# Decoder recurrence on one Trainium2 core: the shifted table of alignments, the place of the state term, and who adds the mask

## The chip, the core and the metric

One NeuronCore of a Trainium2 chip runs the whole program: a chain of eight layers over 16 rows of 128 tokens. The metric is the device time of one execution, in microseconds (us). The change touches only the decoder recurrence, a loop of 128 steps that lie behind each other.

## What is computed

The decoder reads the encoder rows `hbatch` (16 batches, 128 positions) and makes 128 steps. Each step needs the attention weights `alpha` and the state `s` of the step before:

```python
def step(carry, tgt):
    s, c, alpha = carry
    f = lax.conv_general_dilated(alpha, conv_w, (1,), 'SAME', dimension_numbers=('NCH', 'OIH', 'NCH'))
    e = jnp.einsum('a,bta->bt', va, jnp.tanh(enc_proj + (s @ Wa_s.T)[:, None, :] + jnp.einsum('bft,af->bta', f, Wa_f) + ba))
    e = jnp.where(mask, e, jnp.float32(-1e+30))
    alpha_new = jax.nn.softmax(e, axis=1)[:, None, :]
    g = jnp.einsum('bt,btd->bd', alpha_new[:, 0], hbatch)
    y = jnp.tanh(g @ L_gy_w.T + L_gy_b + s @ L_sy.T) @ L_yy_w.T + L_yy_b
    rec = tgt @ L_ys.T + s @ L_ss.T + g @ L_gs_w.T + L_gs_b
    ig, fg, cg, og = jnp.split(rec, 4, axis=1)
    c_next = _sig(fg) * c + _sig(ig) * jnp.tanh(cg)
    s_next = _sig(og) * jnp.tanh(c_next)
    return ((s_next, c_next, alpha_new), y)
```

`conv_w` has 10 filters of 101 taps over the 128 positions; the mask cuts off positions beyond a batch's length. The output `y` is made after the loop from saved states and weights.

## The kernel before, in words

Everything here is in `stage_decoder`. The 16 batches are two groups (`g` = 0, 1) of 8. The loop `steps` runs 64 times over two time steps; a time step is two halves, `half(g, n, o, m, ...)`. In a half, group `g` does the back of its step n (context, gates, state) while the other group `o` does the front of its step (convolution, tanh, energies, softmax). So there are 256 halves, and each group goes round once in two of them. Every engine has its own copy of `half` and runs its instructions in the order in which they are written there; semaphores tie the engines together.

One half, by engine and line of the profile:

- TensorE (PE): `turn_alignment` (L1839) turns the weights `al` of group g into `AT`; `state_term` (L1781) makes `Wa_s` times the state of o into `SW`; `spread_filters` (L1800) adds the 10 filters, spread over 128 channels by `Wa_f`, to the sums that hold the encoder part; `gates_of_context` (L1828) makes the gates of g, in two parts with `mask` (L1808) between them, which starts the energies `E` of o with the mask through an identity matrix in bf16; `energy` (L1815) adds the energies; `turn_gates` (L1835) turns `rec` into `T`; `gates_of_state` (L1821) begins the gates of o; `filter_rows` (L1789) applies the filters of g's next step to the table `hk`, two batches to each of the four 32-column tiles of the array.
- ScalarE (ACT): `keep_filters` (L1883) copies the filtered rows out of PSUM, times `ri`; `squash` (L1893, L1898) is the tanh over 8 batches; `fill` (L1886) puts the encoder part into PSUM for g's next step; L1912 is the tanh of g's gates; `exps` (L1902) is the exponential of the energies of o with its row sum, which a second instruction reads out; L1916 is the tanh of the cell.
- VectorE (DVE): `keep_alignment` (L1990), `keep_state_term` (L1963), `add_state` (L1973), `fill` (L1967), the gate sum `rec` (L2004), `top` (L1980: the negated row maximum of the energies), the cell (L2010, L2012, L2013), `align` (L1984: the reciprocal `ri` of the row sum; L1985: `al` = `ex` times `ri`), and last the state `sT` (L2021).
- SyncE (SP), the DMA queue: it writes the exponentials of o to DRAM, padded with 50 zeros in front (L1748, 4 KB), waits for that to land, and reads them back as the table `hk` (L1750): row t, batch b holds the padded row shifted by t, so that 101 shifted copies (padded to 112 rows) stand under each other and a matmul over the rows is the convolution. In the second time step of an iteration it also loads the next `rin` (L1754).
- GpSimd (POOL) stores weights and states for the output.

The order around the change is thus written out by hand; no planner decides it. The table of o, made from the exponentials of one half, is used by `filter_rows` at the end of the next.

## Time and profile before

| | us |
|---|---|
| median of 3 runs | 4053.48 (4051.23 to 4054.08) |
| the profiled execution, its own time | 4058.55 |
| its span | 4056.8 |
| decoder loop in it, first to last gate tanh | 2201.6 to 3566.0 |

Over the span TensorE is busy 80%, its weight loads 54%, VectorE 55%, ScalarE 39%, GpSimd 12%. The page cuts the span in 40 slices; the decoder loop is slices 22 to 35, in which the granted TensorE clock is 9 tenths or more. Busy shares tell little in such a loop: what counts is which wait ends last in each half. Of a row of the timeline the first number is the start in us from the start of the span, the second how long it took; in square brackets stands the idle time of the engine before it and what ended it.

### The profile page before, as it was taken

The page shows a single profiled execution, that of the slowest core. Times are in us where ns is not written, and L with a number is a line of the kernel's source. Part 1 is how long each engine was busy: PE and PEld are TensorE (multiplying, and loading weights), DVE is VectorE, ACT ScalarE, POOL GpSimd, SP SyncE. Part 2 cuts the span into 40 slices and gives each one's busy share as a digit, 9 for nine tenths or more (in the row PEclk, how much of TensorE's full clock was granted, in tenths as well). Part 3 has the DMA queues.
Part 4 walks back from the last instruction along what each step waited for, and adds up shares of the span by engine and source line. Part 5 has one row for each costly group of instructions (what it writes and reads, how often), then busy time and mean ns, then how long its engine had stood idle before and what let it go on. Part 6 is the DMA issues. An engine that isn't in the chain of part 4 may idle for free. (4 is left out here: it accounts for less than half of the span.)

```text
span 4056.8 us, 109059 instructions
## 1 busy us (share of the span) xinstructions
PE 3261.3 (80%) x43050; PEld 2192.1 (54%) x43122; DVE 2232.7 (55%) x5373; ACT 1577.2 (39%) x3966; POOL 505.4 (12%) x1854
## 2 busy tenths in 40 slices
PE   7556568544489999998598999999999999965998
PEld 4424145322266666666354666666666666623554
DVE  2656767588845555555213555555555555563444
ACT  2221134344422222222112666666666666622222
POOL 0000421233300000000000000000000000033222
PEclk8576689877789999999798999999999999975888
DMA  2000020200010000000101333333333333301000
GB/s 95 3 3 0 10 46 9 86 0 0 0 44 0 0 0 0 0 0 0 52 26 50 90 90 90 90 90 88 91 89 90 90 90 87 93 18 48 25 26 31
DMA packets 278734, 176.56 MB, mean 44 GB/s; under 512 B 14320, under 2 KB 267840, under 8 KB 278608
## 3 DMA queue, kind: packets, MB, share of 16 engines
q1 hardware_dynamic: 275920, 172.57, 14.5%
q0 software_dynamic: 2752, 3.18, 0.5%
q8 instruction: 37, 0.61, 0.1%
q14 instruction: 25, 0.20, 0.0%
HBM read 164.98 MB, written 13.90 MB: 44 GB/s over the span
## 5 line engine op out<-in xcount | busy, mean ns | idle before, releaser
L1828 PE MATMUL ps<-de_hg,st_at 128*32 128x128 f32 x16384 | 516.3, 275 | 0.3 <-DVE st_at L1990 0.3
L1828 PEld LDWEIGHTS ps<-de_hg,st_at 128*32 128x32 f32 x16384 | 424.5, 110 | 31.6 <-DVE st_at L1990 0.5
L1893 ACT ACTIVATE st_th<-ps,st_sw 128x128 f32<-128x128 f32 x1024 | 292.8, 369 | 248.0 <-PE ps L1800 248.0
L1973 DVE TENSOR_TENSOR st_th<-ps,st_sw 128x512 f32<-128x512 f32 x256 | 177.2, 692 | 155.1 <-PE ps L1800 155.1
L1247 PEld LDWEIGHTS ps<-sa_xt,w_wq 128*128 128x128 f32 x2048 | 234.7, 194 | 11.1 <-issue 9.3
L1247 PE MATMUL ps<-sa_xt,w_wq 128*128 128x128 f32 x2048 | 237.9, 278 | 2.0 <-ACT sa_xt L1363 2.0
L1766 POOL COPY de_ah<-st_at 128x8 f32 (+1 forms) x256 | 51.1, 199 | 1507.0 <-DVE st_at L1990 1507.0
L1318 PE MATMUL ps<-sa_wo,sa_ct 128*128 128x512 f32 x512 | 225.0, 598 | 13.1 <-issue 13.1
L1789 PE MATMUL ps<-st_hk,st_cwt 112*32 112x128 f32 x4096 | 164.7, 278 | 84.9 <-DMA st_hk<-padded_alignments 82.9
L2228 PE MATMUL ps<-rf_wb,rf_sp 128*128 128x512 bf16 x737 | 202.2, 434 | 4.7 <-issue 2.9
L1800 PE MATMUL ps<-st_fs,st_waf 32*128 32x128 f32 x4096 | 186.5, 296 | 12.2
L1789 PEld LDWEIGHTS ps<-st_hk,st_cwt 112*32 112x32 f32 x4096 | 100.6, 109 | 149.6 <-ACT st_gt L1912 106.6
L1967 DVE COPY ps<-de_enc 128x512 f32<-128x512 f32 x256 | 175.1, 684 | 5.3 <-PE ps L1862 5.3
L955 PE MATMUL ps<-w_identb,ff_q 128*128 128x128 bf16 x256 | 33.1, 311 | 173.8 <-ACT ff_q L1000 173.8
L2004 DVE TENSOR_TENSOR st_rec<-ps,st_rin 128x128 f32<-128x128 f32 x256 | 74.8, 292 | 176.2 <-PE ps L1828 176.2
L1318 PEld LDWEIGHTS ps<-sa_wo,sa_ct 128*128 128x128 f32 x512 | 96.6, 191 | 135.2 <-issue 135.2
L1815 PE MATMUL ps<-st_th,st_vas 128*32 128x128 f32 x4096 | 165.0, 279 | 1.9 <-ACT st_th L1898 1.9
L1898 ACT ACTIVATE st_th<-st_th 128x512 f32<-128x512 f32 x256 | 165.3, 646 | 0.0
L1886 ACT COPY ps<-de_enc 128x512 f32<-128x512 f32 x256 | 157.1, 613 | 12.9 <-PE ps L1862 12.9
L121 ACT ACTIVATE X<-sa_row,sa_rs_ln 128x1024 f32 (+1 forms) x16 | 19.9, 1242 | 343.0 <-POOL sa_rs_ln L117 343.0
L1800 PEld LDWEIGHTS ps<-st_fs,st_waf 32*128 32x128 f32 x4096 | 137.7, 185 | 26.8 <-ACT st_fs L1883 23.9
L2228 PEld LDWEIGHTS ps<-rf_wb,rf_sp 128*128 128x128 bf16 x768 | 84.2, 113 | 114.1 <-issue 49.9
(410 smaller groups left out, 6456.5 us busy)
## 6 DMA issues: line engine op xcount, KB each, us to landing
st_hk<-padded_alignments SPq DMA_DIRECT2D x254, 448.0 KB, 3.6
X<-in_x_dram SPq DMA_DIRECT2D x16, 512.0 KB, 9.2
out_dram<-X SPq DMA_DIRECT2D x16, 512.0 KB, 2.7
w_wq<-in_Wq_perm_dram SPq DMA_DIRECT2D x1, 4096.0 KB
sa_wo<-in_Wo_perm_dram SPq DMA_DIRECT2D x1, 4096.0 KB, 14.2
gate_inputs<-dp_ro SPq DMA_DIRECT2D x16, 256.0 KB, 2.3
st_rin<-gate_inputs SPq DMA_DIRECT2D x128, 32.0 KB, 3.3
rf_wf<-in_weightT_dram SPq DMA_DIRECT2D x8, 512.0 KB, 4.3
```

The source lines that it names most:

```text
L1247: ins = pe.matmul(ps[:, 6 + c, g * P:(g + 1) * P], wq[:, k, (4 * c + g) * P:(4 * c + g + 1) * P], xt[:, k, :], start=(k == 0), stop=(k == ...
L1318: ins = pe.matmul(ps[:, h, :], ct[:, k // 4, (k % 4) * P:(k % 4 + 1) * P], wo[:, k, h * 512:(h + 1) * 512], start=(k == 0), stop=(k == KH ...
L1789: ins = pe.matmul(F[g][32 * j:32 * j + 32, :], cwt[:, i, :], hk[g][:, 2 * j + i, :], start=(i == 0), stop=(i == 1), tile_position=(0, 32 * ...
L1800: ins = pe.matmul(ps[:, j, c0:c0 + P], waf[32 * j:32 * j + 32, i, :], fs[g][32 * j:32 * j + 32, :], start=False, stop=True, tile_position= ...
L1815: ins = pe.matmul(E[g][32 * j:32 * j + 32, :], vas[:, i, :], th[g][:, 2 * j + i, :], start=False, stop=(i == 1), tile_position=(0, 32 * j) ...
L1828: ins = pe.matmul(R[g][32 * q:32 * q + 32, :], at[g][:, b, :], hg[:, BG * g + b, q * P:(q + 1) * P], start=False, stop=(b == BG - 1), tile ...
L1886: act.copy(sums(g, 0), four(enc[:, BG * g:BG * g + 4, :])).then_inc(filled0[g], 1)
L1893: ins = act.activation(th[g][:, b, :], sums(g, 0)[:, b // 2, (b % 2) * P:(b % 2 + 1) * P], ACT.Tanh, bias=sw[g][:, b:b + 1])
L1898: act.activation(v, v, ACT.Tanh).then_inc(th_done[g], 1)
L1967: dve.tensor_copy(sums(g, 1), four(enc[:, BG * g + 4:BG * g + 8, :])).then_inc(filled1[g], 1)
L1973: dve.tensor_tensor(th[g][:, 4:8, :].rearrange("p (k s) n -> p k s n", s=2), sums(g, 1).rearrange("p k (s n) -> p k s n", s=2), sw[g][:, 4 ...
L2228: ins = pe.matmul(ps[:, 4 + h, :], sp3[:, k, part, m * P:(m + 1) * P], wb[:, m, h * 512:(h + 1) * 512], start=(n == 0), stop=(n == 3 * KH ...
```

## The change

Four edits, all in the decoder loop.

1. The table. `hk` has 128 rows in two blocks of 64. Block r holds the batches 2k + r (k = 0 to 3); row t of it is the padded alignment shifted by 2t, 129 elements long, so that elements s to s + 127 are the shift 2t + s. The filters are stored as 64 rows of even taps and 64 of odd taps for each block. SP fills the table with two DMAs of 64 x 4 pieces of 516 bytes in place of one of 112 x 8 pieces of 512 bytes. `filter_rows` has 16 matmuls over 64 rows in place of 8 over 112, at tile positions (64r, 32j), and writes the two blocks to two PSUM banks; `keep_filters` copies 256 columns in place of 128. The PSUM places of R, T, F, E, AT and SW are dealt out anew.
2. `state_term` stands ahead of `turn_alignment`, and the wait for `al` ahead of both.
3. The mask is added by VectorE: `top` is one `tensor_tensor_reduce` that makes `em` = -(E + mask) in SBUF and its row minimum; `exps` reads `em` from SBUF with scale -1. The matmuls of `mask` go, and `gates_of_context` is one part.
4. `align` is split: `invert` (the reciprocal) stays in its place and has a semaphore of its own, `ri_ready`, for which `keep_filters` waits; the multiplication to `al` now follows the state `sT`.

Two instructions only count a semaphore up (`windows_seen`, `energies_seen`) and carry waits.

```diff
-TAPSA, PADA = 112, 50
+TAPSA, PADA = 128, 50
...
-            cwt = t3.sb("cwt", [TAPSA, 2, 32])
+            cwt = t3.sb("cwt", [P, 2, 32])
...
-            mask16 = t3.sb("mask16", [P, G5, P], BF16)
-            ident16 = t3.sb("ident16", [P, P], BF16)
+            maskf = t3.sb("maskf", [P, G5, P])
...
-            hk = pair("hk", [TAPSA, BG, P])
+            hk = pair("hk", [P, BG // 2, P + 4])
...
+            em = pair("em", [P, P])
...
-            fs = pair("fs", [P, P])
+            fs = pair("fs", [P, 2, P])
...
-            R = [ps[:, 4 + g, 0:P] for g in range(G5)]
-            T = [ps[:, 4 + g, P:2 * P] for g in range(G5)]
-            F = [ps[:, 4 + g, 2 * P:3 * P] for g in range(G5)]
-            E = [ps[:, 6 + g, 0:P] for g in range(G5)]
-            AT = [ps[:, 6 + g, P:2 * P] for g in range(G5)]
-            SW = [ps[:, 6 + g, 3 * P:3 * P + BG] for g in range(G5)]
...
+            R = [ps[:, 4 + 2 * g, 0:P] for g in range(G5)]
+            T = [ps[:, 4 + 2 * g, P:2 * P] for g in range(G5)]
+            F = [ps[:, 4 + 2 * g:6 + 2 * g, 2 * P:3 * P] for g in range(G5)]
+            E = [ps[:, 5 + 2 * g, 0:P] for g in range(G5)]
+            AT = [ps[:, 5 + 2 * g, P:2 * P] for g in range(G5)]
+            SW = [ps[:, 7 - 2 * g, 3 * P:3 * P + BG] for g in range(G5)]
...
-            def hankel(g):
-
-                return bass.AP(pad_d, g * BG * AW, [[1, TAPSA], [AW, BG], [1, P]])
+            def hankel(g, r):
+
+                return bass.AP(pad_d, (g * BG + r) * AW, [[2, 64], [2 * AW, BG // 2], [1, P + 1]])
...
-                        sp.dma_start(cwt[:, i, 16 * i:16 * i + 10], a["conv_wT"]).then_inc(w_load, 16)
+                        for s in range(2):
+                            sp.dma_start(cwt[64 * i:64 * i + 64, s, 16 * i:16 * i + 10],
+                                         a["conv_wT"].rearrange("(t s) c -> s t c", s=2)[s]).then_inc(w_load, 16)
...
@@ -1747,7 +1749,8 @@
                         sp.wait_ge(exp_done[o], m + 1)
                         sp.dma_start(pad_d.ap()[BG * o:BG * o + BG, PADA:PADA + P], ex[o][0:128:16, :]).then_inc(ex_out[o], 16)
                         sp.wait_ge(ex_out[o], 16 * m + 16)
-                        sp.dma_start(hk[o][:, :, :], hankel(o)).then_inc(hk_in[o], 16)
+                        for r in range(2):
+                            sp.dma_start(hk[o][64 * r:64 * r + 64, :, 0:P + 1], hankel(o, r)).then_inc(hk_in[o], 16)
...
                     def filter_rows(g, n):
                         if not isinstance(n, int) or n > 0:
                             pe.wait_ge(gates_done[g], n)
-                            pe.wait_ge(hk_in[g], 16 * n)
-                        for i in range(2):
-                            for j in range(4):
-                                ins = pe.matmul(F[g][32 * j:32 * j + 32, :], cwt[:, i, :], hk[g][:, 2 * j + i, :],
-                                                start=(i == 0), stop=(i == 1), tile_position=(0, 32 * j), skip_group_check=True)
+                            pe.wait_ge(hk_in[g], 32 * n)
+                            pe.sem_inc(windows_seen)
+                        for s in range(2):
+                            for r in range(2):
+                                for j in range(4):
+                                    ins = pe.matmul(F[g][32 * j:32 * j + 32, r, :], cwt[64 * r:64 * r + 64, s, :],
+                                                    hk[g][64 * r:64 * r + 64, j, s:s + P], start=(s == 0), stop=(s == 1),
+                                                    tile_position=(64 * r, 32 * j), skip_group_check=True)
                         ins.then_inc(f_ps[g], 1)
...
-                                                fs[g][32 * j:32 * j + 32, :], start=False, stop=True,
+                                                fs[g][32 * j:32 * j + 32, i, :], start=False, stop=True,
...
-
-                    def mask(g, n):
-                        pe.wait_ge(sw_ready[g], n + 1)
-                        for j in range(4):
-                            pe.matmul(E[g][32 * j:32 * j + 32, :], ident16[:, 32 * j:32 * j + 32], mask16[:, g, :],
-                                      start=True, stop=False, tile_position=(0, 32 * j), skip_group_check=True)
...
-                                                start=False, stop=(i == 1), tile_position=(0, 32 * j), skip_group_check=True)
+                                                start=(i == 0), stop=(i == 1), tile_position=(0, 32 * j), skip_group_check=True)
...
-                    def gates_of_context(g, n, h):
+                    def gates_of_context(g, n):
                         pe.wait_ge(at_ready[g], n + 1)
-                        for b in range(4 * h, 4 * h + 4):
+                        for b in range(BG):
                             for q in range(4):
                                 ins = pe.matmul(R[g][32 * q:32 * q + 32, :], at[g][:, b, :], hg[:, BG * g + b, q * P:(q + 1) * P],
                                                 start=False, stop=(b == BG - 1), tile_position=(0, 32 * q), skip_group_check=True)
-                        if h == 1:
-                            ins.then_inc(r_sum[g], 1)
+                        ins.then_inc(r_sum[g], 1)
...
                     def turn_alignment(g, n):
-                        pe.wait_ge(al_ready[g], n + 1)
                         pe.transpose(AT[g], al[g][:, :], ident[:, :]).then_inc(at_ps[g], 1)
 
                     def half(g, n, o, m, u, more):
                         front = not isinstance(m, int) or m <= LAST
+                        pe.wait_ge(al_ready[g], n + 1)
+                        if front:
+                            state_term(o, m)
                         turn_alignment(g, n)
                         if front:
-                            state_term(o, m)
                             spread_filters(o, m)
-                        gates_of_context(g, n, 0)
-                        if front:
-                            mask(o, m)
-                        gates_of_context(g, n, 1)
+                        gates_of_context(g, n)
                         if front:
...
-                            act.wait_ge(al_ready[g], n)
-                        act.activation(fs[g][:, :], F[g], ACT.Identity, scale=ri[g][:, 0:1]).then_inc(f_kept[g], 1)
+                            act.wait_ge(ri_ready[g], n)
+                        act.activation(fs[g][:, :, :], F[g], ACT.Identity, scale=ri[g][:, 0:1]).then_inc(f_kept[g], 1)
...
-                        act.activation(ex[g][:, :], E[g], ACT.Exp, bias=nm[g][:, 0:1], accum_out=sm[g][:, 0:1]).then_inc(exp_done[g], 1)
+                        act.activation(ex[g][:, :], em[g][:, :], ACT.Exp, bias=nm[g][:, 0:1], scale=-1.0, accum_out=sm[g][:, 0:1]).then_inc(exp_done[g], 1)
...
                     def top(g, n):
                         dve.wait_ge(e_ps[g], n + 1)
-                        dve.tensor_reduce(nm[g][:, :], E[g], AX, ALU.max, negate=True).then_inc(e_max[g], 1)
-
-                    def align(link, g, n):
+                        dve.sem_inc(energies_seen)
+                        dve.tensor_tensor_reduce(em[g][:, :], E[g], maskf[:, g, :], -1.0, 3e38, ALU.add, ALU.min, nm[g][:, :]).then_inc(e_max[g], 1)
+
+                    def invert(g, n):
                         dve.wait_ge(exp_done[g], n + 1)
-                        link(dve.reciprocal(ri[g][:, :], sm[g][:, :]))
+                        dve.reciprocal(ri[g][:, :], sm[g][:, :]).then_inc(ri_ready[g], 1)
+
+                    def align(g, n):
+                        dve.wait_ge(ri_ready[g], n + 1)
                         dve.tensor_scalar(al[g][:, :], ex[g][:, :], ri[g][:, 0:1], None, ALU.mult).then_inc(al_ready[g], 1)
...
                         if front:
-                            align(link, o, m)
+                            invert(o, m)
                         dve.wait_ge(tc_done[g], n + 1)
                         if more:
                             dve.wait_ge(hist_s[g], n + 1)
 
                             dve.scalar_tensor_tensor(out=states(g), in0=to, scalar=1.0, in1=tc[g][:, :], op0=ALU.add,
                                                      op1=ALU.mult).then_inc(st_ready[g], 1)
+                        if front:
+                            align(o, m)
```

TensorE, first half of the loop and the start of the second; `st_` marks the decoder's tiles, `ps` is PSUM. Before:

```order
L1839 MATMUL ps<-identity,st_al 128x128
L1781 MATMUL ps<-st_sT,st_was 128x8
L1800 MATMUL ps<-st_fs,st_waf 128x128 x8
L1828 MATMUL ps<-de_hg,st_at 32x128 x16
L1808 MATMUL ps<-st_mask,st_ident 32x128 x4
L1828 MATMUL ps<-de_hg,st_at 32x128 x16
L1812 ISA
L1815 MATMUL ps<-st_th,st_vas 32x128 x8
L1835 MATMUL ps<-identity,st_rec 128x128
L1821 MATMUL ps<-st_lss,st_sT 32x128 x4
L1786 REGISTER_ALU
L1789 MATMUL ps<-st_hk,st_cwt 32x128 x8
```

The same place of TensorE now:

```order
L1784 MATMUL ps<-st_sT,st_was 128x8
L1837 MATMUL ps<-identity,st_al 128x128
L1806 MATMUL ps<-st_fs,st_waf 128x128 x8
L1828 MATMUL ps<-de_hg,st_at 32x128 x32
L1812 ISA
L1815 MATMUL ps<-st_th,st_vas 32x128 x8
L1834 MATMUL ps<-identity,st_rec 128x128
L1821 MATMUL ps<-st_lss,st_sT 32x128 x4
L1789 REGISTER_ALU
L1794 MATMUL ps<-st_hk,st_cwt 32x128 x16
L1783 REGISTER_ALU
```

The state's product and the transpose have changed places, the mask is gone, the filter has twice the matmuls, and a register instruction now stands ahead of the next state's product.

VectorE, from the gate sum to the end of a half (here group 0 is g and group 1 is o). Before:

```order
L2004 TENSOR_TENSOR st_rec0<-ps,st_rin0 128x128
L1980 TENSOR_REDUCE st_nm1<-ps 128x1
L2010 SCALAR_TENSOR_TENSOR st_c10<-st_gt0,st_cc0 128x8
L2012 SCALAR_TENSOR_TENSOR st_c20<-st_gt0 128x8
L2013 SCALAR_TENSOR_TENSOR st_cc0<-st_c10,st_c20 128x8
L1984 RECIPROCAL st_ri1<-st_sm1 128x1
L1985 TENSOR_SCALAR st_al1<-st_ex1,st_ri1 128x128
L2021 SCALAR_TENSOR_TENSOR st_sT0<-st_gt0,st_tc0 128x8
```

The same place of VectorE now:

```order
L2004 TENSOR_TENSOR st_rec0<-ps,st_rin0 128x128
L1976 ISA st_em1,st_nm1<-ps,st_maskf 128x128
L1976 ISA st_nm1 128x1
L2010 SCALAR_TENSOR_TENSOR st_c10<-st_gt0,st_cc0 128x8
L2012 SCALAR_TENSOR_TENSOR st_c20<-st_gt0 128x8
L2013 SCALAR_TENSOR_TENSOR st_cc0<-st_c10,st_c20 128x8
L1980 RECIPROCAL st_ri1<-st_sm1 128x1
L2021 SCALAR_TENSOR_TENSOR st_sT0<-st_gt0,st_tc0 128x8
L1984 TENSOR_SCALAR st_al1<-st_ex1,st_ri1 128x128
```

The maximum is now two instructions, and the weights `al` stand behind the state.

## Rows read from the trace of the kernel before

**Rows 1.** One line's instructions: the gate tanh, one in each half.

```profile
L1912 ACT ACTIVATE st_gt<-ps x256: 197/198/199, 2201.6 to 3566.0; 128x32 f32<-128x32 f32 x128
```

**Rows 2.** Who waited for whom, 2200 to 3570 us: total us, times, longest.

```profile
PEld ps L1789 <- ACT st_gt L1912: 106.6, 123, 1.2
...
PE ps L1789 <- DMA st_hk<-padded_alignments: 82.9, 131, 1.3
...
PEld ps L1839 <- DVE st_al L1985: 55.7, 140, 1.1
```

**Rows 3.** Timeline of the half from 2711.54 us, cut to one chain.

```profile
2711.54 0.20 ACT L1912 ACTIVATE st_gt<-ps 128x32 f32<-128x32 f32 x1 [0.51 <-PE ps L1835]
...
2712.12 0.58 SPq L1748 DMA_DIRECT2D padded_alignments<-st_ex  x1
...
2712.49 0.64 PE L1789 MATMUL ps<-st_hk,st_cwt 112*32 112x128 f32 x16 [0.63 <-DMA st_hk<-padded_alignments]
...
2713.61 0.73 PE L1800 MATMUL ps<-st_fs,st_waf 32*128 32x128 f32 x16
2713.79 0.31 SPq L1750 DMA_DIRECT2D st_hk<-padded_alignments  x1
```

**Rows 4.** Timeline of the next half, from 2717.16 us, to the one after.

```profile
2717.16 0.20 ACT L1912 ACTIVATE st_gt<-ps 128x32 f32<-128x32 f32 x1 [0.55 <-PE ps L1835]
...
2717.39 0.17 DVE L2010 SCALAR_TENSOR_TENSOR st_c<-st_gt,st_cc 128x8 f32<-128x8 f32 x1 [0.20 <-ACT st_gt L1912]
2717.47 0.16 DVE L2012 SCALAR_TENSOR_TENSOR st_c<-st_gt 128x8 f32<-128x8 f32 x1
2717.48 0.38 PEld L1789 LDWEIGHTS ps<-st_hk,st_cwt 112*32 112x32 f32 x16 [0.27 <-DMA st_hk<-padded_alignments]
...
2717.50 0.20 ACT L1902 ACTIVATION_READ_ACCUMULATOR st_ex<-ps,st_nm 128x1 f32 x1
...
2717.75 0.15 DVE L1984 RECIPROCAL st_ri<-st_sm 128x1 f32<-128x1 f32 x1
2717.87 0.21 ACT L1916 ACTIVATE st_tc<-st_cc 128x8 f32<-128x8 f32 x1 [0.16 <-DVE st_cc L2013]
2717.94 0.29 DVE L1985 TENSOR_SCALAR st_al<-st_ex,st_ri 128x128 f32<-128x128 f32 x1
2718.14 0.17 DVE L2021 SCALAR_TENSOR_TENSOR st_sT<-st_gt,st_tc 128x8 f32<-128x8 f32 x1
2718.20 0.37 ACT L1883 ACTIVATE st_fs<-ps,st_ri 128x128 f32<-128x128 f32 x1
...
2718.28 0.33 PE L1839 MATMUL ps<-identity,st_al 128*128 128x128 f32 x1
2718.36 0.30 PEld L1781 LDWEIGHTS ps<-st_sT,st_was 128*128 128x128 f32 x2
2718.45 0.31 PE L1781 MATMUL ps<-st_sT,st_was 128*128 128x8 f32 x2
...
2718.68 0.73 PE L1800 MATMUL ps<-st_fs,st_waf 32*128 32x128 f32 x16
...
2721.26 0.65 PE L1815 MATMUL ps<-st_th,st_vas 128*32 128x128 f32 x16
...
2721.83 0.33 PE L1835 MATMUL ps<-identity,st_rec 128*128 128x128 f32 x1
...
2722.20 0.20 ACT L1912 ACTIVATE st_gt<-ps 128x32 f32<-128x32 f32 x1 [0.51 <-PE ps L1835]
...
2722.78 0.57 SPq L1748 DMA_DIRECT2D padded_alignments<-st_ex  x1
```

**Rows 5.** The page's DMA issues: KB each, median us from issue to landing.

```profile
st_hk<-padded_alignments SPq DMA_DIRECT2D x254, 448.0 KB, 3.6
...
gate_inputs<-dp_ro SPq DMA_DIRECT2D x16, 256.0 KB, 2.3
```

**Rows 6.** TensorE's timeline of 2712.48 to 2712.56 us alone: the matmuls begun there.

```profile
2712.49 0.32 PE L1789 MATMUL ps<-st_hk,st_cwt 112*32 112x128 f32 x4 [0.63 <-DMA st_hk<-padded_alignments]
```

More of the change, by code:

```diff
@@ L1867, in _ @@
                     spread_filters(0, 0)
-                    mask(0, 0)
                     energy(0, 0)
@@ L2029, in _ @@
                     fill(1, 0)
[L2030 removed]
                     top(0, 0)
[L2032 removed]
+                    invert(0, 0)
+                    align(0, 0)
                     def start(it):
                         state["it"] = it
[L2036 removed]
+                        state["link"] = Chain(dve, dve_seq, it * 2 * U5 * 2)
                     steps(dve, half, start)
```

14 lines of the change are left out of this document (5 added, 9 removed).

## The prediction

> **What bounds the kernel now.** I read the page first, for where the time lies, then the waits of the decoder loop, then the timeline of two halves that follow each other, and last the DMA issues. The loop has 256 gate tanhs, the first at 2201.6 us and the last at 3566.0 [rows 1]: 1364.4 / 255 = 5.35 us for a half. Nothing outside the loop changes but set-up of a few instructions, so one hundredth of a microsecond in every half is 2.56 us.
>
> The waits show that TensorE waits in front of the filter, for the gates 106.6 us and for the table 82.9 us, and for the weights `al` 55.7 us [rows 2]. The timeline tells which of them count. Halves come in pairs. The long half runs from gate tanh to gate tanh in 2717.16 - 2711.54 = 5.62 us [rows 3, 4], the short one in 2722.20 - 2717.16 = 5.04 us [rows 4].
>
> In the long half the filter waits for its table and starts only at 2712.49, 0.95 us after the gate tanh began; the spread of the filters follows at 2713.61 [rows 3]. The table is a ring over two halves: exponentials written at 2712.12, table asked for at 2713.79 (1.67 us later), landing 3.6 us after that [rows 5], filter, copy, spread, tanh, energies, maximum, exponential, and the next write at 2722.78 [rows 4]: 10.66 us with no slack, which is the pair of halves.
>
> In the short half the table is there in time, and another ring bounds it: gate tanh (ends 2717.36), cell, exponential and its sum (ends 2717.70), reciprocal at 2717.75, `al` at 2717.94 to 2718.23, transpose 0.05 us later at 2718.28, spread 0.40 us after that at 2718.68, tanh, energies at 2721.26, gates turned at 2721.83, next gate tanh at 2722.20 [rows 4]. From the spread to the next gate tanh it is 3.52 us here and 3.55 in the long half.
>
> So there are two floors: 5.35 a half by the table's ring, 5.04 by the ring over the gates. The change lowers the first and raises the second.
>
> **The table.** 448 KB become 2 x 64 x 4 x 516 B = 258 KB, from 896 pieces to 512. The nearest row is the store of the gate inputs, 256 KB in pieces of 512 B: 2.3 us to landing [rows 5]. The second DMA is issued about 0.35 us after the first (the issue takes 0.31 [rows 3]), so I take 2.3 + 0.35 = 2.65 us. Bounds: 1.67 (what the 4 KB write takes until the next issue) and 3.6 + 0.35 = 3.95. The Trainium skill, "DMA: Bandwidth & Descriptors", section "Anatomy of one DMA", gives a fixed 2.0 us and bytes over 436 GB/s; by it the table would take 2.6 us and before 3.05. The trace has 3.6 for the latter.
>
> With 2.65 the table's ring is 10.66 - 0.95 = 9.71, plus what the change adds in it: 0.09 for 256 columns in the filter copy, 0.03 for the filter, about 0.10 for the maximum, 0.08 for waits that sit in instructions of their own: 10.0 us, or 5.0 a half. It leaves the path if the other ring is longer.
>
> **The ring over the gates, step by step from the short half [rows 4].** The cell's tanh ends at 2718.08, so the state can start at 2718.11 (it started at 2718.14, behind `al`). `al` now follows it, by the 0.08 us that lie between L2010 and L2012: 2718.19 in place of 2717.94, +0.25 us. It cannot start earlier, since the queue is in order. This is the largest price and nothing hides it: the transpose waited 0.42 us for `al` and started 0.05 us behind it.
>
> The wait for `al` sits, in every other half, in the register instruction ahead of the state's product. In the row of the filter such a wait costs 2717.48 - 2717.36 = 0.12 us against 0.05 for a wait in the load itself: +0.07 in half of the halves, +0.035 on the mean.
>
> The order on TensorE: today transpose and product run in 2718.28 to 2718.76 and the spread starts 0.08 before that end. The product has two weight loads, which together take 0.30 us, and what comes last drains last: the product works on 8 columns, the transpose on 128. With the product first I estimate that the transpose's load starts 0.21 us in (0.30 less the 0.09 by which the product's first load lies ahead of its first matmul, 2718.36 to 2718.45), and the transpose ends 0.33 later, at 0.54 in place of 0.48: +0.07 with rounding up. Bounds: 0, if its load is pulled ahead, and 0.17, the distance between the starts of transpose and product today.
>
> The filter: 16 instructions in a row before (each product passes twice), 32 now, in eight tiles in place of four. Before, four matmuls began so close behind 2712.49 that together they end after 0.32 us, when one alone lasts 0.27 to 0.30 [rows 6]; the sixteen end after 0.64. So the issue is quick, and each tile's four products take their turns, about 0.11 us each. Eight tiles also have four turns, so I take +0.03 us. Bounds: 0, and eight turns in place of four, +0.44. The filter copy takes 256 columns: +0.09. The path by it: gates end 2717.36, hops 0.20, filter 0.67, copy 0.05 + 0.46, next 0.05: the spread could start at 2718.79. By the other path it starts at 2718.19 + 0.29 + 0.05 + 0.47 = 2719.00. So filter and copy lie hidden, with 0.2 us to spare.
>
> The Trainium skill, "TensorE: Matmul & The Clock Gate", section "Wait — 56ns, not 53.3ns?", says that from one matmul's start to the next it is never less than about 25 ns, however small they are. By it the 32 would take 0.8 us of starts in place of 0.4, and the filter path would be 0.4 longer, hence longer than the other by 0.2. This speaks against the change. The four of rows 6 do not bear it out.
>
> The maximum: a second instruction reads out the minimum. The row nearest to it is the exponential's read-out of 0.20 us, beside the 0.08 from L2010 to L2012; I take +0.10 on the exponential. Bounds: 0 and 0.4. The reciprocal then ends at 2718.00 and the state starts at 2718.11 anyhow: hidden for 0.1 us, and to `al` for 0.25. Above that it costs in full, so 0 to 0.15.
>
> The mask: four matmuls and a wait go. The energies begin when the tanh is done (the context's matmuls end by then), and turning the gates follows them by 0.57 us. Neither gets earlier: 0. At best 0.06.
>
> The state's product itself is earlier against the transpose, but who waits for it (tanh and sum, behind the spread) has over 0.5 us to spare: 0. The PSUM places cost nothing that a row shows.
>
> Sum for a half: 5.04 + 0.25 + 0.035 + 0.07 = 5.395, and half of the 0.03 by which the stretch behind the spread differs, 0.015: 5.41. Against 5.35 that is +0.06 us, 256 x 0.06 = +15 us. Then the execution has 4058.55 + 15 = 4073.9; it stands 5.1 above the median of 4053.48, so the median becomes 4069. The gain on every long half (0.2) is paid for by the loss on every short one (0.37).
>
> **Rivals.**
>
> Cheap order (faster). Transpose and product cost the same in either order, the hop is hidden, and the mask gives its 0.06: 5.04 + 0.25 + 0.015 - 0.04 = 5.27 a half, 0.08 less, -20 us, 4033. For it: the loads of the two overlap today, and nobody waits at the product itself. Against: what drains last is wider. It decides if hop and order together cost less than the mask gives back.
>
> Eight turns (slower). The row blocks do not run at once, or the issue is the bound as in the skill's rule: filter +0.44, spread at 2718.79 + 0.41 = 2719.20, 0.20 above the forecast: 5.61 a half, +67 us, 4120. It decides from 0.2 us extra filter on. Against it: rows 6, and the spread, which uses four row blocks with sixteen matmuls in 0.73 us, of which one lasts 0.27 to 0.37.
>
> The table stays late (slower). Two DMAs land as late as one, at 3.95: ring 10.66 + 0.35 + 0.30 = 11.3, 5.65 a half, +77 us, 4130. Against it: 256 KB in 2.3 us.
>
> The change not doing what it says: the waits for the table are simply replaced by idle at the same place with 5.35 a half, 4053. For it nothing but that the two effects are nearly equal.
>
> **Chances.** Forecast 50% (own range 4054 to 4084, by 0.03 us either way on the two small terms), cheap order 25% (4018 to 4048), eight turns 11%, table late 5%, no change 9%. A change within 0.2% (8 us) is about what cannot be told from none. Same: 0.13 of the forecast, whose range begins inside that bound, and the 0.09 of no change, 0.22. Faster: the cheap order and 0.01 of the forecast, 0.26. Slower: what is left of the forecast, 0.36, and the two slow rivals, 0.16, together 0.52. The range 4022 to 4118 leaves out a tenth at either end: the best of the cheap order, and the larger part of the slow rivals.
>
> **What would show it.** In the profile after: no TensorE wait for `st_hk` in the loop, landing 2.3 to 3.0 us; `al` starting behind `sT` by under 0.1 us; TensorE idle before the state's product, ended by `al`; halves of one length, near 5.4, in place of pairs of 5.04 and 5.62; spread 0.47 us behind the product's start; the filter's 32 matmuls in about 0.67 us. The prediction is wrong if halves are at 5.3 or less, if the filter takes over 0.9 us, or if ScalarE's filter copy ends what TensorE waits for ahead of the spread.

## The result, and the profile after

The changed kernel takes 4127.26 us (median of 4 runs, 4125.05 to 4134.6), the kernel before 4052.36 in the same comparison: ratio 1.0188, 95% interval 1.017 to 1.0205. Forecast were 4069 us and a range up to 4118.

The gate tanhs, one in each half (lines view; the row of before is in [rows 1]):

```profile
L1908 ACT ACTIVATE st_gt<-ps x256: 198/198/199, 2205.4 to 3630.3; 128x32 f32<-128x32 f32 x128
```

(3630.3 - 2205.4) / 255 = 5.588 us for a half against 5.35, and 256 x 0.238 = 61 us of the 68 between the spans of the two profiled executions (4124.4 against 4056.8). The time is lost in the loop.

Who waited for whom, 2200 to 3640 us (total us, times, longest); it answers to [rows 2]:

```profile
PEld ps L1794 <- issue: 163.9, 254, 1.9
...
PE ps L1794 <- DMA st_hk<-padded_alignments: 99.5, 210, 1.7
PEld ps L1784 <- DVE st_al L1984: 49.1, 122, 0.6
PEld ps L1806 <- ACT st_fs L1879: 47.4, 170, 0.4
```

The wait that was to vanish has grown: 99.5 us for the table in 210 halves, against 82.9 in 131. Behind it the spread (L1806) waits for the filter copy, 47.4 us. The prediction named both as signs of its failure.

One ring through the table in the changed kernel's timeline (start, duration, engine, line, operation; in brackets the idle time and what ended it); [rows 3, 4] are its like:

```profile
2715.74 0.62 SPq L1750 DMA_DIRECT2D padded_alignments<-st_ex  x1
...
2715.90 0.17 DVE L2021 SCALAR_TENSOR_TENSOR st_sT<-st_gt,st_tc 128x8 f32<-128x8 f32 x1
2715.99 0.28 DVE L1984 TENSOR_SCALAR st_al<-st_ex,st_ri 128x128 f32<-128x128 f32 x1
...
2717.46 1.26 SPq L1753 DMA_DIRECT2D st_hk<-padded_alignments  x2
...
2721.25 0.67 PE L1794 MATMUL ps<-st_hk,st_cwt 64*32 64x128 f32 x32 [0.24 <-DMA st_hk<-padded_alignments]
...
2722.02 0.47 ACT L1879 ACTIVATE st_fs<-ps,st_ri 128x256 f32<-128x256 f32 x1 [0.40 <-PE ps L1794]
...
2722.62 0.73 PE L1806 MATMUL ps<-st_fs,st_waf 32*128 32x128 f32 x16
...
2725.19 0.64 PE L1815 MATMUL ps<-st_th,st_vas 128*32 128x128 f32 x16
...
2726.07 0.29 DVE L1976 CUSTOM_DVE_ANT_0 st_em<-ps,st_maskf 128x128 f32<-128x128 f32 x1 [0.48 <-PE ps L1815]
...
2726.28 0.08 DVE L1976 DVE_READ_ACCUMULATOR2_ANT st_nm<- 128x1 f32 x1
...
2726.40 0.41 ACT L1898 ACTIVATE st_ex<-st_em,st_nm 128x128 f32<-128x128 f32 x1
...
2726.92 0.62 SPq L1750 DMA_DIRECT2D padded_alignments<-st_ex  x1
```

From store to store 11.18 us for two halves, 5.59 each, where it was 10.66. The two table issues keep SyncE's queue for 1.26 us, and the filter starts 3.79 us behind the first (2717.46 to 2721.25). The DMA issues (line, durations of one issue in ns min/median/max; then from issue to landing):

```profile
L1753 SPq DMA_DIRECT2D st_hk<-padded_alignments x508: 582/613/1095, 2199.7 to 3617.1; - x170
...
DMA to landing us min/median/max: 2.8/3.0/4.4
```

Each issue takes 0.61 us where the one of before took 0.31 [rows 3], and each 129 KB land 3.0 us after it. The second issue starts 0.64 us behind the first, so the table is complete 0.64 + 3.0 = 3.64 us behind the first issue (3.67 by the median of all): the 3.6 of before [rows 5] is not undercut at all.

### The profile page after: what moved, and what is told of

Same layout as the page of the kernel before. It is cut to its first block and busy times, and to the rows that moved or that the text cites. A ratio compares the mean times of both kernels' runs of the same rounds, so it can differ in the third digit from the quotient of the medians.

```text
span 4124.4 us, 116046 instructions
## 1 busy us (share of the span) xinstructions
PE 3303.4 (80%) x46194; PEld 2185.7 (53%) x46194; DVE 2239.2 (54%) x5628; ACT 1629.2 (40%) x3966; POOL 501.8 (12%) x1854
## 5 line engine op out<-in xcount | busy, mean ns | idle before, releaser
L1828 PE MATMUL ps<-de_hg,st_at 128*32 128x128 f32 x16384 | 502.0, 275 | 0.3 <-DVE st_at L1989 0.3
L1828 PEld LDWEIGHTS ps<-de_hg,st_at 128*32 128x32 f32 x16384 | 432.9, 110 | 31.5 <-DVE st_at L1989 0.5
L1794 PE MATMUL ps<-st_hk,st_cwt 64*32 64x128 f32 x8192 | 171.7, 274 | 103.1 <-DMA st_hk<-padded_alignments 99.5
L2230 PE MATMUL ps<-rf_wb,rf_sp 128*128 128x512 bf16 x768 | 211.7, 443 | 0.9 <-DVEq L2350 0.9
L1806 PE MATMUL ps<-st_fs,st_waf 32*128 32x128 f32 x4096 | 186.5, 296 | 15.1 <-ACT st_fs L1879 0.8
L1794 PEld LDWEIGHTS ps<-st_hk,st_cwt 64*32 64x32 f32 x8192 | 110.8, 105 | 164.7 <-issue 164.7
L1879 ACT ACTIVATE st_fs<-ps,st_ri 128x256 f32<-128x256 f32 x256 | 121.9, 476 | 145.2 <-PE ps L1794 145.1
L1806 PEld LDWEIGHTS ps<-st_fs,st_waf 32*128 32x128 f32 x4096 | 137.7, 185 | 57.9 <-ACT st_fs L1879 47.4
```

Source lines behind the costliest of these rows:

```text
L1794: ins = pe.matmul(F[g][32 * j:32 * j + 32, r, :], cwt[64 * r:64 * r + 64, s, :], hk[g][64 * r:64 * r + 64, j, s:s + P], start=(s == 0), st ...
L1806: ins = pe.matmul(ps[:, j, c0:c0 + P], waf[32 * j:32 * j + 32, i, :], fs[g][32 * j:32 * j + 32, i, :], start=False, stop=True, tile_positi ...
L1828: ins = pe.matmul(R[g][32 * q:32 * q + 32, :], at[g][:, b, :], hg[:, BG * g + b, q * P:(q + 1) * P], start=False, stop=(b == BG - 1), tile ...
L2230: ins = pe.matmul(ps[:, 4 + h, :], sp3[:, k, part, m * P:(m + 1) * P], wb[:, m, h * 512:(h + 1) * 512], start=(n == 0), stop=(n == 3 * KH ...
```

## The experiments

Two theories. **A**: the ring through the table sets the time (its landing, and what the mask adds in it). **B**: the new orders set it, through the ring over the gates. "Half" below is the mean from gate tanh to gate tanh, worked out as above from the two ends of that line. Ratios are to the kernel before on the same chip, in brackets the 95% interval.

**Half a table.**

```
-                        for r in range(2):
+                        for r in range(1):
...
-                            pe.wait_ge(hk_in[g], 32 * n)
+                            pe.wait_ge(hk_in[g], 16 * n)
```

> The changed kernel, in which only the first of the two shifted-table DMAs of each half is issued and waited for; the rows that the second fills keep old data, so that part of the filters' computation is left out. Theory A (the ring through the shifted table sets the time, because the second issue comes about 0.6 us behind the first and lands last): the table is complete about 0.6 us earlier, two halves per ring give -0.3 us each until the gates' ring of about 5.4 us per half takes over, so 5.59 - 0.18 = 5.41 per half and 4127 - 46 = about 4080 us. Rival B (the new order of the alignment behind the state and of SW ahead of AT sets the time): no change, 4120 to 4130. Rival C (the first DMA also becomes slower or faster when alone): the landing differs from 3.0 us.

Measured: 4079.39 us, 1.0046 [1.0029, 1.0063]. Its gate tanhs, and its waits:

```profile
L1908 ACT ACTIVATE st_gt<-ps x256: 197/198/198, 2203.5 to 3586.1; 128x32 f32<-128x32 f32 x128
```

```profile
PE ps L1784 <- DVE st_al L1984: 86.4, 252, 0.4
...
PE ps L1794 <- DMA st_hk<-padded_alignments: 1.9, 7, 0.5
```

The wait for the table is gone (1.9 us), TensorE now waits for `al` in every half, and a half is 1382.6 / 255 = 5.422 us. That is the ring over the gates by itself; the prediction had worked it out as 5.41. A holds, and B, which had no change here, does not.

**The mask back on TensorE** (the rest as changed).

```
-  dve.tensor_tensor_reduce(em[g][:, :], E[g], maskf[:, g, :], -1.0, 3e38, ALU.add, ALU.min, nm[g][:, :])
+  dve.tensor_reduce(nm[g][:, :], E[g], AX, ALU.max, negate=True)
...
```

The four matmuls of the mask come back between two parts of the context's gates, and the exponential reads PSUM again.

> The changed kernel with the mask put back on TensorE (four identity matmuls between the two halves of the gates' context) and the maximum as a plain tensor reduction; table and order stay changed. Theory A (table ring sets the time, and the mask on VectorE adds 0.165 us from energies to exponential and 0.037 us in the exponential to it): 0.2 us less per ring of two halves, 5.59 - 0.10 = 5.49 per half, about 4127 - 26 = 4101 us. Rival B (order): no change or slower by up to 0.25 us per half for the four matmuls back before the gates' sum.

Measured: 4105.04 us, 1.0105 [1.0089, 1.0122]; half 5.51. The mask costs 0.08 us a half, 20 us, as A has it (26 were forecast). Two halves of this execution, 8.28 and 7.66 us long, ran in part at the lower granted clock, half of full speed; without them a half is 5.49, the figure of the forecast.

**The orders back**, VectorE's alone, and both. With both, SW's place in PSUM is moved to match; it then lies in the bank in which the gates' sum runs, so that part of that sum may be changed, and TensorE waits for SW's copy ahead of the context's gates.

```
                         if front:
                             invert(o, m)
+                            align(o, m)
...
-                        if front:
-                            align(o, m)
```

> The changed kernel with the alignment put back ahead of the state on VectorE, all else as changed (TensorE still waits for the alignment ahead of SW and AT). Theory A (table ring): the alignment is not on the table's ring, whose data go from the exponential to the padded copy; no change, 4120 to 4135. Rival B (the alignment behind the state costs 0.25 us per half on the gates' ring and that ring sets the time): 5.59 - 0.2 = 5.39 per half, about 4075.

> The changed kernel with both orders put back: alignment ahead of the state on VectorE, AT ahead of SW on TensorE (SW sits in the other bank of its pair so that it doesn't share one with the running gates' sum, and TensorE waits for its copy). Theory A (table ring): 4115 to 4130, no more than 12 us from the changed kernel. Rival B (order on the gates' ring): near the kernel before, 4050 to 4060.

Measured: 4126.49 us, 1.0156 [1.0139, 1.0173], and 4126.78 us, 1.016 [1.0143, 1.0177]; both 5.58 a half, where the changed kernel has 5.59. (The ratios are 0.3% lower than its 1.0188 because the kernel before stood at 4062 on this chip and at 4052 on the other; the changed kernel was not run on both.)

The first of the two does not decide between A and B, since its edit does not shorten the ring over the gates. One half of it:

```profile
2711.45 0.20 ACT L1908 ACTIVATE st_gt<-ps 128x32 f32<-128x32 f32 x1 [0.51 <-PE ps L1834]
...
2712.45 0.28 DVE L1984 TENSOR_SCALAR st_al<-st_ex,st_ri 128x128 f32<-128x128 f32 x1
2712.65 0.17 DVE L2022 SCALAR_TENSOR_TENSOR st_sT<-st_gt,st_tc 128x8 f32<-128x8 f32 x1
2712.87 0.30 PEld L1784 LDWEIGHTS ps<-st_sT,st_was 128*128 128x128 f32 x2 [0.32 <-DVE st_sT L2022]
```

With the mask on VectorE the exponential and the reciprocal are 0.2 us late, so the alignment starts 1.00 us behind the gate tanh (1.04 in the changed kernel, 0.79 in the one before) and pushes the state to 1.20. The state's product, which needs both, gains nothing: it starts 1.42 and 1.51 us behind the gate tanh by turns, against 1.45 and 1.37 in the kernel with half a table, whose order is the changed one. The second run does decide: there the transpose comes first, in every other half 1.34 us behind the gate tanh (1.61 in the changed kernel), and the time stays. In the changed kernel the order is not on the path, and B falls with it, as it did with half a table.

**Each part alone in the kernel before**: the mask, and the order.

> The kernel before with only the mask changed: the four identity matmuls go, VectorE adds the mask and takes the maximum in one operation, and the exponential reads the masked energies. The old table and both old orders stay. Theory A (the ring through the table sets every second half; the new operation starts 0.16 us behind its wait and is followed by a read of its result, 0.165 us in all, and the exponential takes 0.037 us longer): 0.2 us per ring of two halves, 0.10 us per half by 256 halves, +26 us, ratio 1.006. Rival (what the changed kernel shows there belongs to its other changes): no change, or faster by up to 0.035 us per half, 9 us, for the matmuls that go.

> The kernel before with only the order changed: the alignment behind the state on VectorE, SW ahead of AT on TensorE, the reciprocal released on its own. Old table, old mask. Theory A (two rings; the table's takes 10.66 us per two halves and doesn't pass the alignment, the gates' takes 5.04 us per half and gets 0.25 + 0.035 us longer, 5.33 us, still under 5.35): 0 to 5 us slower, ratio 1.000 to 1.001. Rival (the alignment's delay is paid in every second half, as those halves wait for nothing else): 0.28 x 128 = 36 us slower, ratio 1.009. Rival (state ahead is worth something): faster by up to 0.3%.

Measured: mask 4080.46 us, 1.0049 [1.0033, 1.0066]; order 4079.67 us, 1.005 [1.0031, 1.0068].

```profile
L1903 ACT ACTIVATE st_gt<-ps x256: 197/198/198, 2204.0 to 3587.5; 128x32 f32<-128x32 f32 x128
```

```profile
L1914 ACT ACTIVATE st_gt<-ps x256: 197/197/198, 2203.7 to 3587.2; 128x32 f32<-128x32 f32 x128
```

Both kernels have 5.425 us a half, and for different reasons: with the mask the long and short halves remain (on the mean 5.52 to 5.57 and 5.27 to 5.30), with the order all are 5.40 to 5.44. The expectation for the order left out the 0.07 us of the product ahead of the transpose, which the prediction had; with it, about 5.40 a half. Each of the two edits costs 0.075 us a half with the old table in place. The mask costs on both rings: the short halves, 5.04 in the kernel before, become 5.25 (median), because `al` starts 1.00 us behind the gate tanh in place of 0.79 when it still stands ahead of the state.

**What makes the table late.** Row length: rows of 128 elements in place of 129.

> The changed kernel with table rows of 128 elements (512 bytes) in place of 129 (516 bytes); the last column that the odd taps read keeps old data, so one position of the filters is computed wrongly. All else as changed. Theory A1 (the row of 516 bytes is what makes an issue last 0.61 us and a DMA of 129 KB land only after 3.0 us): the issue falls to about 0.31 us as in the kernel before, the second one starts 0.3 us earlier and both land 0.3 to 0.6 us earlier, so the gates' ring of 5.42 us per half takes over: about 4080 us. Theory A2 (the shape of the transfer, 64 partitions by 4 rows, or a source that steps by two elements, makes it slow): issue 0.61 us, landing 3.0 us, time 4120 to 4130.

Measured: 4117.29 us, 1.0136 [1.0118, 1.0155]; issue 0.612 us, landing 3.0, half 5.546. The issue does not hang on it. The landing does a little: by the median of all rings the table is complete 3.58 us behind the first issue in place of 3.67, and 0.09 us over two halves is the 0.04 us that a half is shorter.

Gaps between the rows in SBUF, taken out of the changed kernel and put into the one before (`hk` pitch 132 to 129, and 128 to 132).

> The changed kernel with the table's rows laid close in SBUF, 129 elements apart in place of 132, so that the four rows of a partition are one contiguous piece in the destination as the eight rows are in the kernel before. Nothing is left out. Theory P (the gaps in the destination are what makes an issue last 0.61 us): the issue falls to about 0.31 us, the second one starts and lands 0.3 us earlier, the ring of 11.18 us per two halves falls by at least 0.3 us, 0.15 us per half, 38 us: about 4089 us, ratio to the kernel before about 1.008. Rival (the issue's length is set by something else, such as the source): issue 0.61 us, 4120 to 4130 us, ratio 1.016 to 1.019.

> The kernel before with its table rows laid 132 elements apart in SBUF in place of 128; still one DMA of 112 partitions by 8 rows of 512 bytes. Theory P: the issue rises from 0.31 to about 0.6 us and the first packet and the landing come about 0.3 us later, the ring 10.66 + 0.3 = 10.96 us per two halves, 0.13 to 0.15 us per half, +33 to +38 us, ratio 1.008 to 1.010. Rival: issue 0.31 us, landing 3.6 us, no change.

Measured: 4119.27 us, 1.0164 [1.0147, 1.0181], issue 0.612, landing 3.1; and 4063.68 us, 1.0016 [1.0006, 1.0027], issue 0.308, landing 3.6. The gaps are not the cause.

The step of two, taken out of the changed kernel and put into the one before.

```
-  [[2, 64], [2 * AW, BG // 2], [1, P + 1]]
+  [[1, 64], [2 * AW, BG // 2], [1, P + 1]]
```

> The changed kernel with table rows that start one element apart in the source in place of two; 64 partitions by 4 rows of 516 bytes, two issues, as changed. The filters then get windows that their weights don't belong to, so the attention's location features are computed wrongly; the number and shape of instructions stay. Theory S (the step of two in the source makes an issue last 0.61 us): issues of about 0.31 us, the second 0.3 us earlier, the last landing 0.3 to 0.6 us earlier; ring 11.18 - 0.3 to 0.6, 5.44 to 5.42 us per half, 4080 to 4090 us, ratio 1.005 to 1.008. Theory N (the number of partitions sets it): issues stay at 0.61 us, no change against the changed kernel, ratio 1.016 to 1.019.

> The kernel before with table rows that start two elements apart in the source (padded rows in DRAM 112 elements longer so that no window leaves its row); one DMA of 112 partitions by 8 rows of 512 bytes. The filters get every second window, so the location features are computed wrongly; instructions stay. Theory S: the issue rises from 0.31 to about 0.6 us, the landing from 3.6 to about 3.9 us, ring +0.3 us, +0.13 us per half, ratio 1.008. Theory N: issue 0.31 us, landing 3.6 us, no change.

Measured: 4125.98 us, 1.0183 [1.0165, 1.02], issue 0.612; and 4072.57 us, 1.0047 [1.003, 1.0064], issue 0.308 with a landing of 3.7. The step isn't what lengthens the issue, but in the kernel before it costs about 0.1 us of landing.

The number of partitions, alone, in the kernel before.

> The kernel before with its table DMA cut to the first 64 partitions by 8 rows of 512 bytes, source step one; the other 48 rows keep zeros, so the taps from 65 on are left out. Theory S (step): issue 0.31 us, and by the packets (512 in place of 896) a landing of 3.0 to 3.2 us, 0.4 us or more off the ring: up to 0.15 us per half faster, as far as the gates' ring of 5.04 us lets it: 4015 to 4035 us, ratio about 0.993. Theory N (partitions): issue 0.6 us, landing 3.6 to 3.7 us as for the 64 rows two elements apart, no change, ratio 1.000 to 1.004.

Measured: 4067.45 us, 1.0032 [1.0017, 1.0047]. The table's issues here:

```profile
L1750 SPq DMA_DIRECT2D st_hk<-padded_alignments x254: 594/600/697, 2199.6 to 3559.8; - x127
...
DMA to landing us min/median/max: 3.4/3.6/4.0
```

Of the edits of one thing, this is the one that turns 0.308 into 0.600. Three sevenths of the bytes are gone, and it lands no earlier: the first packet comes 1.40 us behind the issue in place of 0.97, and what fewer packets save is lost again.

**Split, and one issue.** The kernel before with its table cut in two DMAs of 56 partitions, and with 64 rows two apart in one DMA.

> The kernel before, with its one table DMA of 112 partitions by 8 rows of 512 bytes cut into two of 56 partitions, issued one behind the other; nothing else changed. If a second issue as such costs what the changed kernel shows (0.61 us each and the last landing 3.65 us behind the first issue): the last landing stays near the 3.6 us of the one DMA, no change within 0.3%. If each issue stays at 0.31 us and the fixed part of a landing (the 0.96 us up to the first packet, and what lies behind the last) is paid from the second issue: the last landing is 0.1 to 0.35 us later, the ring 10.66 + 0.35 = 11.0 us at most, up to 0.17 us per half, ratio up to 1.011. If the split halves the time of the packets: no slower than before.

> The kernel before with a table of 64 rows two elements apart, 129 elements long and laid close, all eight batch elements of a half in the same 64 partitions and in one DMA (258 KB in place of 448 KB, 512 rows in place of 896); the filters take 16 matmuls, four deep on each of four column tiles. Old mask, old order. The filters' pass, two deep in 0.64 us before, is expected to take about 1.25 us, +0.6 us in the ring. Theory B1 (a landing shrinks with its packets; by 384 packets of 27 ns on 16 engines 0.65 us, to about 3.0 us): ring 10.66 + 0.6 - 0.6 = 10.66, time 0 to 10 us from the kernel before, ratio 0.998 to 1.003. Theory B2 (the landing's fixed part dominates and it stays near 3.5 us): ring 11.2, 5.6 us per half, +64 us, ratio 1.016.

Measured: 4179.07 us, 1.0297 [1.028, 1.0315], half 5.80; and 4137.55 us, 1.0206 [1.0189, 1.0224], half 5.62. The split misses every branch of its expectation. By the medians of all rings the last packet comes 3.29 us behind the first issue (2.91 before) and the filter starts 4.27 behind it (3.74 before). Its issues:

```profile
L1751 SPq DMA_DIRECT2D st_hk<-padded_alignments x508: 307/397/468, 2196.3 to 3666.9; - x170
```

That accounts for some 0.5 of the 0.91 us that its pairs of halves grew by (2 x 5.804 - 10.70). The rest is the clock. In 34 of its halves the granted TensorE clock falls to half of full speed, 1.2 GHz, for a part of the half; in the loop of the kernel before it never does. One of them, as rows of the timeline (and, last, of the windows view: the stretch, busy time of PE, PEld, DVE, ACT and POOL, granted clock, DMA share, GB/s):

```profile
2313.25 0.65 PE L1790 MATMUL ps<-st_hk,st_cwt 112*32 112x128 f32 x16 [1.26 <-DMA st_hk<-padded_alignments]
...
2314.37 1.24 PE L1801 MATMUL ps<-st_fs,st_waf 32*128 32x128 f32 x16
2315.54 1.94 PE L1829 MATMUL ps<-de_hg,st_at 128*32 128x128 f32 x32
```

```profile
2314.40:2317.80 3.40, 3.40 (x64) 2.98 (x67) 1.37 (x3) 2.06 (x6) 0.33 (x2) 0.50 0.67 145
```

The spread takes 1.24 us where it takes 0.73 at the full clock. Before the clock fell, TensorE had waited 1.26 us for the table; the other long halves have waits of up to 1.4 us too, so what decides is not shown. The 34 halves last 7.79 us on the mean, the other 91 long ones 6.06: 34 x 1.73 = 59 us, 0.46 us a pair. So about half of what the split costs is its landing, and the other half is the clock.

With one DMA of 64 rows the landing is 3.7 us at an issue of 0.600, and the filter, four matmuls deep, takes 1.08 us: 0.44 more than before, and this is the slower branch.

**56 rows in place of 64 in the changed kernel.** The 101 taps need 51 rows, so nothing is left out.

```
-  [[2, 64], [2 * AW, BG // 2], [1, P + 1]]
+  [[2, 56], [2 * AW, BG // 2], [1, P + 1]]
...
-  sp.dma_start(hk[o][64 * r:64 * r + 64, :, 0:P + 1], hankel(o, r))
+  sp.dma_start(hk[o][64 * r:64 * r + 56, :, 0:P + 1], hankel(o, r))
```

> The changed kernel with 56 rows of the table for each half of the partitions in place of 64; the 101 taps need 51 of them and the weights of the rest are zeros, so nothing is left out. Theory D (56 partitions from partition 0 issue in 0.31 us, as in the kernel before cut in two): the second issue starts 0.3 us earlier and lasts 0.46 us, the last landing comes 0.3 us earlier, ring 11.18 - 0.3 = 10.88, 5.44 us per half, about 4089 us, ratio 1.009. Rival (the last landing is as late as in the kernel before cut in two, 4.07 us behind the first issue, in place of 3.65): ring 11.6, 5.8 us per half, 4180 us, ratio 1.03; in between if the landing grows by less.

> As the kernel with 56 rows, and with the mask back on TensorE. By the sum of the parts 0.1 us per half less than the kernel with 56 rows, as far as the gates' ring of 5.42 us lets it: 4080 us (ratio 1.006) by theory D, 4155 us (1.025) by the rival.

Measured: 4085.72 us, 1.0078 [1.0061, 1.0094], and with the mask on TensorE 4087.2 us, 1.0079 [1.0061, 1.0096]. Issues, gate tanhs and waits with 56 rows:

```profile
L1753 SPq DMA_DIRECT2D st_hk<-padded_alignments x508: 307/366/1292, 2202.2 to 3576.4; - x170
...
L1908 ACT ACTIVATE st_gt<-ps x256: 197/198/198, 2207.6 to 3589.2; 128x32 f32<-128x32 f32 x128
```

```profile
PE ps L1784 <- DVE st_al L1984: 87.4, 251, 1.4
...
PE ps L1794 <- DMA st_hk<-padded_alignments: 1.9, 4, 0.9
```

Eight partitions fewer in each DMA bring 1.1% (ratio 1.0188 to 1.0078). The two issues now take 0.31 and 0.42, and the last packet comes 2.31 us behind the first issue in place of 3.14; how much of that is the issues and how much the eighth of the packets that is gone was not taken apart. The half is 5.418 us, the gates' ring again, which is why the mask no longer matters.

**With VectorE's order put back as well**: 56 rows, mask on TensorE, alignment ahead of the state, SW still ahead of AT.

> The changed kernel with 56 rows for each table DMA, the mask back on TensorE and the alignment back ahead of the state on VectorE; SW stays ahead of AT on TensorE, as the two-bank sum of the filters leaves no other bank for it. The table's ring is then about 11.18 - 0.2 - 0.3 or more = 10.4 to 10.68 us per two halves, 5.2 to 5.34 us per half. The gates' ring: SW again starts about 0.08 us earlier, at 1.29 us behind the gates' tanh, the spread 0.48 us behind it, so 5.42 - 0.08 = 5.34 us per half. Forecast: 5.34 us, level with the kernel before (5.35), ratio 0.999 to 1.001. Rival (the mask and the alignment, still waiting for a semaphore between reciprocal and product, keep the gates' ring at 5.42 us): ratio 1.006. Rival (the ring loses the whole 0.25 us of the alignment): 5.2 us per half, ratio 0.991.

Measured (median of 11 executions): 4048.35 us, 0.9974 [0.9964, 0.9983], faster than the kernel before and than the changed one.

```profile
L1920 ACT ACTIVATE st_gt<-ps x256: 197/198/198, 2206.1 to 3555.5; 128x32 f32<-128x32 f32 x128
```

```profile
PEld ps L1785 <- DVE st_al L1996: 66.5, 126, 0.5
PEld ps L1785 <- DVE st_sT L2034: 45.3, 126, 0.4
...
PE ps L1795 <- DMA st_hk<-padded_alignments: 1.8, 2, 1.3
```

Its timeline in one half:

```profile
2715.08 0.20 ACT L1920 ACTIVATE st_gt<-ps 128x32 f32<-128x32 f32 x1 [0.55 <-PE ps L1842]
...
2715.87 0.29 DVE L1996 TENSOR_SCALAR st_al<-st_ex,st_ri 128x128 f32<-128x128 f32 x1
...
2716.07 0.17 DVE L2034 SCALAR_TENSOR_TENSOR st_sT<-st_gt,st_tc 128x8 f32<-128x8 f32 x1
...
2716.29 0.30 PEld L1785 LDWEIGHTS ps<-st_sT,st_was 128*128 128x128 f32 x2 [0.36 <-DVE st_sT L2034]
2716.29 0.39 PE L1785 MATMUL ps<-st_sT,st_was 128*128 128x8 f32 x2
```

The half is 1349.4 / 255 = 5.292 us, 0.14 below the 5.432 that it had with the same table and mask; 0.08 were forecast. The alignment starts 0.79 us behind the gate tanh in place of 1.04 (by the median of the halves), the state 0.99 in place of 0.95. So of the 0.25 us, 0.14 come back. The rest does not, because the product now stands ahead of the transpose and needs the state, which ends 1.16 us behind the gate tanh where `al` ends at 1.07. The short halves of the kernel before have `al` and state at these same places and last 5.04 us; the like halves here last 5.24, since the spread starts 1.74 us behind the gate tanh in place of 1.53. That 0.20 us is the price of TensorE's new order once VectorE's is the old one.

In one more kernel, the changed one with the gaps taken out and the mask on TensorE together, the time is 4103.71 us, 1.012 [1.0104, 1.0137], as with the mask alone.

## Why the prediction was wrong

**The two floors.** Right. Table's ring and gates' ring are what the time goes by in every kernel here but the split one, where the clock adds its part. The direction, slower, came true for another reason than the one given: the forecast had the table off the path and the ring over the gates at 5.41, 0.06 above the 5.35 of before; measured, the table's ring itself grew to 5.59.

**The table's landing: the step that failed.** "I take 2.3 + 0.35 = 2.65 us" became 0.64 + 3.0 = 3.64. The row it was taken from, 256 KB in 2.3 us, is another shape of transfer, and the issue of the same line in another shape (0.31 us for 112 partitions) was taken for the new one. The term is a microsecond too small for two halves: the ring came out at 11.18 in place of 10.0, 5.59 in place of 5.0 a half, and stayed on the path. The figures of the Trainium skill ("DMA: Bandwidth & Descriptors", section "Anatomy of one DMA") that the prediction sets beside it are fitted there to DMAs issued from GpSimd, while these are issued from SyncE; for 129 KB they give an estimate of 2.3 us, and the trace has 3.0. 256 x (5.59 - 5.41) = 46 us; the measured distance from the forecast is 58. Of the other 12, 5 are what the prediction took off because the profiled execution of before stood above its median, which that of the changed kernel does not, and 3.8 the later begin of the loop (2205.4 against 2201.6). With the table made early (half a table, 56 rows) the changed kernel takes 4079 and 4086, inside the range.

**The additions to the table's ring**, by medians of all rings: from the energies to the exponential 0.17 more (0.10 in the forecast), because the custom operation, whose wait stands in an instruction ahead of it, starts 0.16 us later behind the energies; its read-out of 0.08 begins before its end and adds 0.01. The exponential 0.04 (not in the forecast); the filter copy 0.11 (0.09); the filter 0.06 with its wait (0.03 and part of the 0.08); from the store to the first table issue 0.05 (not in it); from that issue to the filter 0.05, 3.74 to 3.79 (forecast -0.95). Sum 0.48, and the ring from 10.68 to 11.17.

**The filter in eight tiles.** Right: 32 matmuls in 0.67 us. "Eight turns" does not come true. Nor does the rule that the prediction cites from the Trainium skill, of at least 25 ns from start to start, which would make 0.8 us of starts: the 32 matmuls of the trace start within 0.40 us.

**The gates' ring at 5.41.** Right, 5.422 and 5.418 in the two kernels that it bounds, and right term by term. `al` starts 0.09 us behind the state (2715.90 to 2715.99, forecast 0.08). With half a table the product starts 1.45 us behind the gate tanh in every other half and 1.37 in the rest, the wait in an instruction of its own (0.08, forecast 0.07). The order on TensorE was priced at 0.07: `al`'s end to the spread is 0.53 us in those halves that are free of that wait, where it was 0.46. The mask on VectorE costs this ring nothing (5.418 with it, 5.432 without), but only because `al` stands behind the state; ahead of it, in the kernel before, it costs the short halves 0.21 us.

**The rivals.** "The table stays late", 3.95 us and 4130, was the case, at 5%. That its 4130 meets the 4127 so closely is in part luck: it has the landing 0.3 us too late and the additions about 0.14 too small. The bound of 3.95 in the working was nearer than the value taken. Against it I had set one row, of another shape; for it stood the table's own row.

## What to carry to other kernels

Price a DMA by a row of its own shape, and above all by the same number of partitions; bytes and packets that go are no gain while issue and landing stay. Where two rings set the time in turn, both must be computed for every edit, since an edit that is free on the one can be paid in full on the other. Before a run is taken as a test of one ring, check in its trace that its edit shortened that ring: putting VectorE's order back did not, as long as the mask kept the alignment late. Of a change made of three parts, run each alone: here the mask and the order each cost 0.5% with the old table, and the table with 56 rows, with only TensorE's new order beside it, is 0.3% faster than the kernel before. The table of 56 rows by itself was not run. By the 0.20 us above, TensorE's order is the next thing to undo; the one kernel that did put SW where the gates' sum runs, so this is not shown to work.

## What the runs showed of the hardware

The issue of a table DMA on SyncE's queue takes 0.308 us from 112 partitions, 0.31 from 56 beginning at partition 0, 0.42 to 0.46 from the second DMA of 56, which begins further up and follows directly on the first (the two were not told apart), and 0.600 to 0.617 from 64, whatever the step, row length or gaps. The first packet comes 0.91 to 0.97 us after the issue begins where the issue is short, and 1.37 to 1.40 where it is long. Why 64 is slow was not found; no other number was tried.

Two DMAs of 56 partitions have their last packet at 2.31 us with 4 rows each, and at 3.29 us with 8 rows each, where one DMA of all 112 partitions by 8 rows has it at 2.91. Only for the latter were one and two compared. In both, the records show 14 small completion packets for each DMA and 16 for the others, so a DMA of 56 partitions seems to be spread over 14 engines.
